# A graph transformer on one core: numerators a slab later, edge transfers in tiles of 128, the counting loop in pairs of groups with slots from registers

## The reference

```python
# layer 0, graph attention: 4 heads of 64 over HID = 256
xl, xr = x @ W_down @ Wl, x @ W_down @ Wr
msg = xl[src] + xr[dst]
act = jnp.where(msg > 0, msg, 0.2 * msg)
e = jnp.einsum('ehd,hd->eh', act, att)          # one score per edge and head
# ... softmax of e over the edges of a dst, weighted sum of xl[src], @ W_up
# both layers, linear attention: 16 heads of 64
q, k, v = elu(x @ Wq + bq) + 1, elu(x @ Wk + bk) + 1, x @ Wv + bv
kv, ksum = k.T @ v, k.sum(rows)                  # per head, over all nodes
out = ((q @ kv) / (q @ ksum + 1e-6)) @ Wo        # numerators over denominators
```

## Time and profile before

| | us |
|---|---|
| median of 3 runs (lowest, highest) | 3459.63 (3458.82, 3460.22) |
| the profiled execution, its span | 3469.89, 3468.2 |
| PE busy, PEld busy | 2749.8 (79%), 2534.2 (73%) |
| DVE, ACT, POOL busy | 1617.4 (47%), 870.3 (25%), 916.4 (26%) |
| granted PE clock, mean | 0.875 |
| stage projection, counting | 62 to 125, 129.6 to 402 |
| mix0, out0, gat | 402 to 929, to 1171, to 1410 |
| gate0 to experts, norm2 and sage0 | to 1890, to 2234 |
| mix1, out1, the rest | to 2643, to 2800, to 3468 |

### The profile page before, as it was taken

How to read it: one execution, slowest core, us unless ns; L and a number is a source line. 1 busy time by engine, 2 the same in 40 slices (tenths; PEclk the granted TensorE clock), 3 DMA queues, 4 the chain that set the end, 5 groups by cost and what they waited for, 6 DMA issues and landing times. The chain is left out here.

```text
span 3468.2 us, 53667 instructions
## 1 busy us (share of the span) xinstructions
PE 2749.8 (79%) x19204; PEld 2534.2 (73%) x19204; DVE 1617.4 (47%) x3435; ACT 870.3 (25%) x1619; POOL 916.4 (26%) x790
## 2 busy tenths in 40 slices
PE   4757587887686399459994999899998979996468
PEld 3534487887676398358884999899997969995257
DVE  6668455455553388465555222233334322224445
ACT  3100132332210156215432100134342120002033
POOL 0166476677656322112210000000000001000154
PEclk7978798998888689659996999899998989997579
DMA  9722333332364696517745211110112461114064
GB/s 225 189 67 68 88 87 87 79 90 73 91 149 104 149 220 167 173 44 202 202 121 140 76 40 40 52 51 26 51 45 81 127 179 56 58 59 138 2 226 148
DMA packets 251509, 370.39 MB, mean 107 GB/s; under 512 B 64744, under 2 KB 193792, under 8 KB 250095
## 3 DMA queue, kind: packets, MB, share of 16 engines
q1 hardware_dynamic: 187457, 287.84, 29.4%
q0 software_dynamic: 63888, 80.33, 10.1%
HBM read 279.45 MB, written 99.41 MB: 109 GB/s over the span
## 5 line engine op out<-in xcount | busy, mean ns | idle before, releaser
L308 PE MATMUL mix_bank<-mix_wkv_hi,layer_act_hi 128*125 128x256 f32 x1280 | 359.4, 281 | 0.0
L309 PE MATMUL mix_bank<-mix_wkv_lo,layer_act_hi 128*125 128x256 f32 x1280 | 359.3, 281 | 0.0
L310 PE MATMUL mix_bank<-mix_wkv_hi,layer_act_lo 128*125 128x256 f32 x1280 | 359.0, 280 | 0.0
L498 POOL DMA_INDIRECT scores<-edge_e,edge_now x170 | 218.2, 1284 | 233.0 <-issue 162.9
L486 POOL DMA_INDIRECT edge_gl<-xl,edge_now x170 | 212.0, 1247 | 171.6 <-issue 169.5
L309 PEld LDWEIGHTS mix_bank<-mix_wkv_lo,layer_act_hi 128*125 128x125 f32 x1280 | 237.7, 186 | 0.1
L310 PEld LDWEIGHTS mix_bank<-mix_wkv_hi,layer_act_lo 128*125 128x125 f32 x1280 | 237.7, 186 | 0.0
L308 PEld LDWEIGHTS mix_bank<-mix_wkv_hi,layer_act_hi 128*125 128x125 f32 x1280 | 237.3, 185 | 0.1
L486 POOL DMA_INDIRECT edge_gr<-xr,edge_now x170 | 214.7, 1263 | 51.9 <-issue 34.8
L308 PE MATMUL out_bank<-out_w_hi,layer_act_hi 128*125 128x256 f32 x640 | 191.1, 299 | 36.5 <-DVE out_w_lo L1617 26.2
L775 PE MATMUL count_pa<-count_hot_s,count_hot_d 125*125 125x416 bf16 (+1 forms) x624 | 146.1, 388 | 68.6 <-DVE count_hot_s L718 66.6
(11 more groups left out here) (509 smaller groups left out, 7654.8 us busy)
## 6 DMA issues: line engine op xcount, KB each, us to landing
ffn_raw<-in_L_ffn_w_dram SPq DMA_DIRECT2D x16, 2048.0 KB
scores<-targets_hole SPq DMA_DIRECT2D x40, 546.9 KB
gat_sc<-scores SPq DMA_DIRECT2D x10, 2187.5 KB
block_raw<-in_L_ffn_W_dram SPq DMA_DIRECT2D x16, 1024.0 KB
norm_x<-x SPq DMA_DIRECT2D x30, 448.0 KB
mix_raw<-in_L_mix_w_qkv_dram SPq DMA_DIRECT2D x24, 512.0 KB
sage_cnt<-at SPq DMA_DIRECT2D x20, 546.9 KB
out_part<-mixt SPq DMA_DIRECT2D x16, 625.0 KB, 4.6
```

The costliest lines, as they stand in the source:

```text
L308: pe.matmul(out, lhs[0], rhs[0], start=first, stop=False)
L309: pe.matmul(out, lhs[0], rhs[1], start=False, stop=False)
L310: return pe.matmul(out, lhs[1], rhs[0], start=False, stop=last)
L498: pool.indirect_dma_start(self.scores, bass.IndirectOffsetOnAxis(ap=self.now[:, u % (2 * RING), 2, j:j + 1].bitcast(U32), axis=0), self.e[ ...
```

## The change

Edges come in tiles of 128: 166 columns of 128, and a last batch of two columns that holds the two edges left and repeats 126 edges of the first two columns (`ET` = 168, 84 batches, 504 indirect transfers instead of 510). A row of xl and xr has 260 instead of 256 elements (`ROW`): the projection adds 0.2·att·x of each head as four linear terms (tables `slope`, `lin`, a PSUM tile `plin`, six small matmuls and one small ACT copy a tile), att is scaled by 0.8, and the edge step becomes add, max(x, 0)·att in one instruction, sum, and an addition of 4 elements a row. Scores stay in `e` for all columns. `now` and its copies go; transfers take their index column from `idx` at fixed addresses, and POOL's loops are written out. The index arrays are loaded in 8 transfers instead of 2. Gathers of b+2 go ahead of scatters, and in counting scatters lag eight batches behind (`LAG`), so that POOL waits for the fill and writes the diagonal only after the gathers of batches 0 to 9; in batches 19 to 25 two batches are scattered at once until the lag is one.

The counting loop has two one-hot pairs a turn (85 groups, 188 pairs for this `dst`), and the slot of four is (base + i) % 2 and j: a register in the addresses of DVE's two outputs and PE's two inputs.

`mix_phase` is one flat list over all slabs, written out for each engine without a loop: n0 to n2 of a slab stand behind the next slab's q0, q1 and q2 follow kv9, w4 and w5 come ahead of pair and w0 to w3 behind it, and wq is loaded first. Each slab's numerators are stored a slab later. The biases' two columns are made once for all slabs. A new semaphore (`s_read`) keeps ACT from writing q0's chunk while the last slab's numerators still read it. gat reads the first 256 elements of xl's rows.

```diff
 EDGES = 21250
-ET = EDGES // R
+EDGE_COLS = EDGES // P
+EDGES_LEFT = EDGES - P * EDGE_COLS
 EB = 2
-BATCHES = ET // EB
+BATCHES = -(-EDGE_COLS // EB) + 1
+ET = EB * BATCHES
 RING = 3
-AHEAD = 3
-COUNT_BATCHES = 6 * RING
+AHEAD = 2
+LAG = 8
+COUNT_BATCHES = 18
 DEEP = 4
-SLAB_BATCHES = 2 * RING
+SLAB_BATCHES = 6
 MIX_END = COUNT_BATCHES + SLAB_BATCHES * (D // (2 * HD))
-PAIRS = ET // 2
+PAIRS = EDGES // (2 * R)
 KH = HID // P
 XW = HD + 2
+ROW = HID + HEADS
+SLOPE = 0.2
...
-                    link(dve.tensor_tensor(self_[:, :], out[:, t % 2, 0:HID], out[:, t % 2, HID:], ALU.add))
-                    link(dve.scalar_tensor_tensor(self_[:, :], self_[:, :], 0.2, self_[:, :], ALU.mult, ALU.max))
-                    link(dve.tensor_tensor(self_[:, :], self_[:, :], attb[:, :], ALU.mult))
-                    link(dve.tensor_reduce(loops[:, t, :], self_[:, :].rearrange("p (a d) -> p a d", a=HEADS), AX.X, ALU.add))
+                    link(dve.tensor_tensor(self_[:, :], out[:, t % 2, 0, :], out[:, t % 2, 1, :], ALU.add))
+                    link(dve.scalar_tensor_tensor(self_[:, 0:HID], self_[:, 0:HID], 0.0, attb[0:R, :], ALU.max, ALU.mult))
+                    link(dve.tensor_reduce(loops[:, t, :], self_[:, 0:HID].rearrange("p (a d) -> p a d", a=HEADS), AX.X, ALU.add))
+                    link(dve.tensor_tensor(loops[:, t, :], loops[:, t, :], self_[:, HID:], ALU.add))
...
+                    act.activation(out[:, t % 2, :, HID:], plin[t % 2][:, 0:2 * HEADS].rearrange("p (j h) -> p j h", j=2), ACT.Copy,
+                                   scale=rms[:, t:t + 1])
+                    act.activation(out[:, t % 2, :, 0:HID], bank[t % 4][0:R, :].rearrange("p (j n) -> p j n", j=2), ACT.Copy,
+                                   scale=rms[:, t:t + 1]).then_inc(s_xo, 1)
...
+                    if t >= 2:
+                        pe.wait_ge(s_xo, t - 1)
                     n = slice(t * R, (t + 1) * R)
+                    for k in range(KH):
+                        mm3(pe, plin[t % 2][:, 0:2 * HEADS], (d_hi[:, k, n], d_lo[:, k, n]), (lin_hi[:, k, :], lin_lo[:, k, :]),
...
     def sync(self, sp):
+        most = P - EDGES_LEFT
         for j, a in enumerate((self.src, self.dst)):
-            sp.dma_start(self.idx[:, j, :], a.rearrange("(p k) -> p k", p=R)).then_inc(self.s_idx, 16)
-        sp.dma_start(self.attb[:, :], self.att.rearrange("(o h) d -> o (h d)", o=1).to_broadcast([R, HID])) \
+            cols = a[0:P * EDGE_COLS].rearrange("(p k) -> p k", p=P)
+            left = a[P * EDGE_COLS:EDGES].rearrange("(p k) -> p k", k=1)
+            sp.dma_start(self.idx[:, j, 0:EDGE_COLS], cols).then_inc(self.s_idx, 16)
+            sp.dma_start(self.idx[0:most, j, EDGE_COLS:ET], cols[0:most, 0:EB]).then_inc(self.s_idx, 16)
+            for k in range(EDGE_COLS, ET):
+                sp.dma_start(self.idx[most:P, j, k:k + 1], left).then_inc(self.s_idx, 16)
+        sp.dma_start(self.attb[:, :], self.att.rearrange("(o h) d -> o (h d)", o=1).to_broadcast([P, HID])) \
...
+    def gather(self, pool, b, j):
+        slot = b % RING
+        if b >= RING and j == 0:
+            pool.wait_ge(self.s_e, b - RING + 1)
+        for row, (buf, x) in enumerate(((self.gl, self.xl), (self.gr, self.xr))):
+            pool.indirect_dma_start(buf[:, slot, j, :], None, x, self.at(row, EB * b + j)).then_inc(self.s_g[slot], 16)
+
+    def scatter(self, pool, b, j):
+        if j == 0:
+            pool.wait_ge(self.s_e, b + 1)
+        k = EB * b + j
+        pool.wait_ge(self.s_sc, 16 * (T + 1) + 16 * k)
+        pool.indirect_dma_start(self.scores, self.at(2, k), self.e[:, k, :], None).then_inc(self.s_sc, 16)
...
+    def written(self, b):
+
+        return max(0, b + 1 - max(1, LAG - max(0, b - COUNT_BATCHES)))
 
     def gpsimd(self, pool, first, end):
-
-        def batch(b, u, last=False):
-            if not last:
-                pool.wait_ge(self.s_now, b + 3)
-            pool.wait_ge(self.s_e, b + 1)
+        if first == 0:
+            pool.wait_ge(self.s_cell, 1)
+            for b in range(AHEAD):
+                for j in range(EB):
+                    self.gather(pool, b, j)
+        for b in range(first, end):
+            done = range(self.written(b - 1) if b else 0, self.written(b))
+            if 0 in done:
+                self.diagonal(pool)
             for j in range(EB):
-                pool.wait_ge(self.s_sc, self.stored(b, j))
-                pool.sem_inc(self.s_turn, 1)
-                pool.indirect_dma_start(self.scores, bass.IndirectOffsetOnAxis(
-                    ap=self.now[:, u % (2 * RING), 2, j:j + 1].bitcast(U32), axis=0),
-                    self.e[:, u % RING, j, :], None).then_inc(self.s_sc, 16)
-                if not last:
-                    self.gather(pool, b + 2, (u + 2) % RING, (u + 2) % (2 * RING), j)
...
         link = Link(dve, e.s_link, 3 * b + 3)
-
-        dve.wait_ge(e.s_turn, EB * RING + EB * (b - RING + 1) + 1)
-        if self.g is not None or u + AHEAD < BATCHES:
-            e.columns(dve, b + AHEAD, (u + AHEAD) % (2 * RING))
         gl, gr = e.gl[:, slot, :, :], e.gr[:, slot, :, :]
-        turn = b // RING if self.g is None else self.first // RING + self.g * (SLAB_BATCHES // RING) + u // RING
-        dve.wait_ge(e.s_g[slot], 32 * EB * (turn + 1))
+        score = e.e[:, b * EB:b * EB + EB, :]
+        dve.wait_ge(e.s_g[slot], 32 * EB * (b // RING + 1))
         link(dve.tensor_tensor(gl, gl, gr, ALU.add))
-        link(dve.scalar_tensor_tensor(gl, gl, 0.2, gl, ALU.mult, ALU.max))
-        link(dve.tensor_tensor(gl, gl, e.attb[:, :].unsqueeze(1).to_broadcast([R, EB, HID]), ALU.mult))
-        dve.tensor_reduce(e.e[:, slot, :, :], gl.rearrange("p t (a d) -> p t a d", a=HEADS), AX.X, ALU.add) \
-           .then_inc(e.s_e, 1)
+        link(dve.scalar_tensor_tensor(gl[:, :, 0:HID], gl[:, :, 0:HID], 0.0,
+                                      e.attb[:, :].unsqueeze(1).to_broadcast([P, EB, HID]), ALU.max, ALU.mult))
+        link(dve.tensor_reduce(score, gl[:, :, 0:HID].rearrange("p t (a d) -> p t a d", a=HEADS), AX.X, ALU.add))
+        dve.tensor_tensor(score, score, gl[:, :, HID:], ALU.add).then_inc(e.s_e, 1)
         self.u += 1
...
 HOTS_DEEP = 4
-GROUPS = (2 * PAIRS + HOTS_DEEP - 1) // HOTS_DEEP
-LAID = GROUPS * HOTS_DEEP // 2
+GROUPS = PAIRS
...
                     with dve.Fori(0, num) as i:
-                        for j in range(TURN):
-                            q = (lo + i) * (TURN // 2) + j // 2
-                            dve.wait_ge(s_used, TURN * (base + i) + j + 1)
-                            dve.tensor_scalar(hot_d[:, j, :], node[:, 0:R], local[:, t, j % 2, bass.ds(q, 1)], None,
-                                              ALU.is_equal)
-                            dve.tensor_scalar(hot_s[:, j, :], node[:, :], ends[:, 0, j % 2, bass.ds(q, 1)], None,
-                                              ALU.is_equal).then_inc(s_hot, 1)
+                        slot = (base + i) % (TURN // 2)
+                        for j in range(2):
+                            dve.wait_ge(s_used, 2 * (base + i) + j + 1)
+                            dve.tensor_scalar(hot_d[:, j, bass.ds(slot, 1), :], node[:, 0:R].unsqueeze(1),
+                                              local[:, t, j, bass.ds(lo + i, 1)], None, ALU.is_equal)
+                            dve.tensor_scalar(hot_s[:, j, bass.ds(slot, 1), :], node[:, :].unsqueeze(1),
+                                              ends[:, 0, j, bass.ds(lo + i, 1)], None, ALU.is_equal).then_inc(s_hot, 1)
                     while todo.u < COUNT_BATCHES * t // (T - 1):
                         todo.step()
...
+EDGE_AFTER = (("q", 0), ("kv", 1), ("kv", 4), ("kv", 7), ("q", 1), ("q", 2))
+W_ORDER = (4, 5, 0, 1, 2, 3)
...
+    flat = [(-1, "w", c) for c in W_ORDER]
+    for g in range(SLABS):
+        flat += [(g, "q", 0)]
+        flat += [(g - 1, "n", j) for j in range(NC) if g]
+        flat += [(g, "kv", t) for t in range(T)] + [(g, "q", 1), (g, "q", 2)]
+        flat += [(g, "w", c) for c in W_ORDER[:2] if g + 1 < SLABS] + [(g, "pair", 0)]
+        flat += [(g, "w", c) for c in W_ORDER[2:] if g + 1 < SLABS]
+    flat += [(SLABS - 1, "n", j) for j in range(NC)]
+    units = [("q", 0)] + [("kv", t) for t in range(T)] + [("q", 1), ("q", 2)]
...
+                    if g:
+                        for j, (o, n) in enumerate(CHUNKS):
+                            sp.wait_ge(s_num, NC * (g - 1) + j + 1)
+                            sp.dma_start(mixt[(g - 1) * P:g * P, o:o + n], num[:, j, 0:n]).then_inc(s_st[j], 16)
...
+                    dve.tensor_scalar(bias_less[:, :], bias_q[:, :], -1.0, None, ALU.mult)
+                    dve.tensor_scalar(bias_more[:, :], bias_q[:, :], 1.0, None, ALU.add).then_inc(s_both, 1)
...
+                for i in range(len(flat) + 2):
+                    if i < len(flat):
+                        start(*flat[i])
+                    first = 2 <= i and flat[i - 2][1] == "pair"
+                    if first:
```

(46 more changed lines are left out.)

458 lines of the change are left out of this document (212 added, 246 removed).

## The result

The changed kernel takes 3296.58 us (median of 4 runs, 3289.06 to 3299.44) against 3459.93 (4 runs, one more than in the table of before): ratio 0.9524, 95% interval 0.9508 to 0.9541. Forecast were 3276, with 3225 to 3350 as the range. The profiled run is 3296.0 with a span of 3294.3; the forecast for it was 3286. So half of the miss is the sum's, and half is that the profiled run of before stood 10.3 above its median and that of after does not.

A forecast was written before the change was run, and what follows sets the result against it. Waits, not a full engine, were taken to hold the stages. Counting -58, mix0 -77, out0 -49, mix1 -5 and projection +5 sum to -184: 3286 us profiled, 3276 for the median, range 3225 to 3350 (0.83).

The forecast's parts named there:

- The price of a transfer: POOL's edge transfers: 128 rows cost 1.01 + 0.30 = 1.31 us each, against 1.23 and 0.30 between for 125 rows.
- Rival B: A 128-row transfer costs POOL what a 125-row one does (1.53 us): mix0 -46, out0 -45, total 3311; chance 0.16.
- What removed the stops: mix0: numerators behind the next slab's q0 have w0 to w3 and q0 as cover, so stops of 9.57 us go.
- The slab: mix0: slabs from 65.2 to 52.2 us, POOL 23 late from the lag's return; 852 instead of 929, -77.
- Counting: Counting stage: fill wait -24, fewer one-hots -15, cheaper edge steps -9, stage end -10; together -58 us.
- rival C: Counting loop bound by its sequencers: 1.03 us a one-hot, +41 instead of -15, total 3332; chance 0.12, with Rival B 0.07.
- The -24 for the fill: Counting: with scatters lagging eight batches, DVE's waits of 4.82, 12.54 and 6.57 us for the zero fill go.
- out0: Stage out0: POOL's 102 transfers at 1.31 us and scatter waits give 193 instead of 242 us, -49 (ends -60, -30).
- mix1: Stage mix1, same new order without edges: less waiting before the last pair and in each slab, -5 us (ends -10, +6).
- rival D: mix0's stops come back, edge steps waiting for gathers delaying w0 to w3: 4 us a slab, total 3304; chance 0.13.
- Projection: Projection stage: six tiny matmuls and one small ACT copy more a tile, +5 us (ends 0, +8).
- Rival E: Slower: transfers over 16 queues keep POOL as long as the long 4 KB ones, 3568 at halfway; chance 0.04.

The follow-up runs named there:

- e2: The changed kernel with edge tiles of 125 rows (510 transfers), all else as in it: 3385.81 us, 0.9779 of the kernel before.
- e4: The changed kernel with LAG = 4 instead of 8, given back in batches 7 to 9, inside counting: 3261.69 us, 0.9412 of the kernel before.
- e1: The changed kernel with numerators n0 to n2 at the end of their own slab, behind w3: 3300.02 us, 0.9537 of the kernel before.
- e12: The changed kernel with tiles of 125 rows and LAG = 4 given back in counting, third occasion: 3350.55 us, 0.9641 of the kernel before.
- e6: The changed kernel with the old counting loop, four one-hot pairs a turn in fixed slots (208 pairs), second occasion: 3432.29 us, 0.9888 of the kernel before.
- e11: The same edit as e6 (counting loop in fours) on the changed kernel, run again on the third occasion: 3433.97 us, 0.9867 of the kernel before.
- e3: The changed kernel with LAG = 1 instead of 8, scatters following their batch at once: 3273.78 us, 0.9452 of the kernel before.
- e9: The changed kernel itself, unedited, run again on the third occasion: 3429.68 us, 0.9876 of the kernel before.

## Why the prediction was right, and what in it was not

**The price of a transfer** was the step that carried the case, and it held: 1.01 + 0.30 taken from 4 KB rows of another stage, 0.97 + 0.30 measured, so the size of a row is not POOL's. Rival B, 125-row price, was e2: but I gave it +35 and it is +89. B's mix0 was too cheap: -46 was taken, -10 measured. So was its out0, which I put at 4 us over the sum's; 102 transfers at 0.22 more are 22 by the sum's own terms, and e2 has 34. I had POOL 55 us late in all; e2's mix0 is 83 us over that of e4, where POOL is never late (517.3 and 434.0), 40 of them in the one slab that takes the lag's return.

**What removed the stops.** The prediction laid them to the numerators' move behind q0, with w0 to w3 as part of the cover. For mix0 that step was wrong, though the stops went and the slab came out right, which is luck in part. e1 shows that the move gives nothing there; e2 and e12 show that the price doesn't either, since with transfers of 1.23 us and gathers that come late (105 us of waits in e2) the only numerator that waits for sums_lo is the last, 4.7 and 4.9 us. What is left is the order within the slab. In the kernel before, the edge step stood between the sums and their lo part on DVE, and of the 8 us before 602.37 its wait was 5.14 and its work 2.78; the changed order has that step ahead of w4, w5 and pair, so that sums_lo follows 0.4 us behind the last sum, as the rows of e1 show, and puts w0 to w3 behind pair. The prediction doesn't name the step's new place; it only takes 2 us for a sums_lo with nothing in its way. No run separates the two halves. By these rows the step is an estimated 7.9 of the 9.57 us of a stop and 1.7 are left for w0 to w3 to cover, near the 1.9 us of each stop in e1's mix1, where there is neither an edge step nor work of w0 to w3 on PE. By e2 and e12 the rest of the change takes mix0 from 527 to 517 us with the lag of 8 and to 474 with a lag of 4 given back in counting, and the tiles of 128 rows take 60 and 40 more (517.3 to 457.1, and 474.3 to 434.0, the latter across two occasions).

**The slab**: 52.2 forecast, 52.7 measured; POOL's lateness by the lag's return 23, measured 21.8 in the second slab and 1.4 in the third. The 7 us missing in mix0 are 0.5 a slab (the wait of 0.71 us for w3 behind pair, which I had at nothing) and the last slab, 57.0 us from its q0 instead of 51.4: it holds two slabs' numerators. The first slab, 49.8, holds none and gives 2.4 back.

**Counting** is the term that was mis-sized, -48 for -58. From a tile's first one-hot to its last, nine stretches add up to 154.2 us before (208 pairs, 0.741) and 144.2 after (188, 0.767): -10 for -15, rival C's mechanism at a tenth of its size on the average (0.03 us a pair for 0.29); by e6 and e11 even these 10 us are not shown to come from the fewer pairs. The rest of the loop went from 87.8 to 58.1, -30 for -33, and the end behind the last one-hot from 29.6 to 21.2, -8 for -10. The -24 for the fill was put on the lag; e3 shows that 14.7 of the 23.9 go without it, by faster transfers and gathers that go ahead of scatters.

**out0** is -47 for -49. **mix1** is -9 for -5, and here the deferral is the cause, by e1. Of the 5.9 us of gat to sage0, for which the sum had nothing, 3.8 are mix1's own start: from PE's first matmul there to DVE's first weights it is 4.0 us instead of 7.8. The changed kernel loads wq first; that this is the cause is not shown. Of rival D only mix0's second slab has anything, the gathers coming in time in its others. The Trainium skill's page "Runtime: NRT & Kernel Launch" ("Instruction fetch mechanics") would let the seven returns of mix1's loop cost something; mix1 gained 8.9 us with its loop gone, but by its waits of PE 6.7 of q_lo, 2.6 of wq_lo and 2.2 of kv_lo went and 1.8 of sums_lo came, which leaves nothing for the returns; and e1, which has no loop there either, takes the 414.7 us of the kernel before. For this loop the trace does not agree. The prediction's other rule from the Trainium skill, how many DMA engines a transfer of 125 or 128 rows uses ("DMA: Bandwidth & Descriptors", "Why a DMA increments its semaphore by 16 and not by 1"), no run here shows: the packets of POOL's queue fell from 63888 to 36432, but a count of packets doesn't say on which engines they ran.

**Projection** +5.7 for +5, but the first one-hot comes at 130.5 to 140.6 us in e1 to e4 and e9, which all have the same projection, so it confirms nothing.

**Not foreseen** is that the gain depends on the occasion: 3430 us against 3297. The forecast is right for the result's occasion and would have been 154 us off on the third. Rival E had transfers over more queues turn against the kernel, but through POOL's own time, which did not move.

## What to carry to other kernels

Ask of each part of a combined change what remains of it when one other part is undone: here the part that gave the change its name is worth nothing in mix0, where the prediction counted on it, and 9 us in mix1, and a tile of three more rows is worth over half (89 of 163 us). Look also for what moved without being named, here an edge step that no longer stands between two links of a chain. A deferral has to be paid back somewhere, so give it back where the deferred engine idles: 4 batches of lag, returned inside counting, beat 8 returned in mix0 by 35 us, of which the traces give 23 to mix0 and 7 to counting. Time a kernel that leans on dense indirect transfers on more than one occasion, with the old one beside it, before trusting its size; and when an order is put back for an experiment, put back its waits too.

## What the runs showed of the hardware

By the medians an indirect transfer of 128 rows cost POOL 0.95 to 0.99 us (the result, e1, e3 to e11) and one of 125 rows 1.21 to 1.23 (the kernel before, e2, e12), with rows of 1 KB or of 16 bytes, on every occasion on which each was traced. On two of three occasions the kernels with 128-row transfers had pauses, most of them under 1 us, between matmuls that wait for nothing, and starts of DVE and ACT up to 10 us late and more, in the stages with edge transfers and nowhere else; for the changed kernel that is 133 us by the medians. e12, the one with 125 rows, had one pause of 1.2 us, and the kernel before, which has no trace of these occasions, was 12 and 15 us slower. Whether it is the chip (8 against 2 and 11) or something else of the occasion, and what the pauses wait for, the runs don't say. For a kernel that must do well everywhere, 125 rows with a lag of 4 (3350 us on the third occasion) is the safer of the two, and e4 (3262 us on the first) the faster; e4 was not run on the other occasions, nor e12 on the first.
